# An attention and mixture-of-experts layer: heads in row groups of 32 partitions, the first batch projected in place, and the experts' down projections as plain fp32 matmuls

## The reference

```python
Q, K, V = (proj(Wq, bq), proj(Wk, bk), proj(Wv, bv))        # 16 heads of 8
scores = jnp.einsum('bhqd,bhkd->bhqk', Q, K) * scale
attn = jax.nn.softmax(scores, axis=-1)
...
shared_out = jax.nn.silu(xf @ sw1) * (xf @ sw3) @ sw2
s = jax.nn.sigmoid(xf @ router_w.T)                          # top 2 of 8, gates from s
h = jax.nn.gelu(jnp.einsum('nd,edh->neh', xf, ew1), approximate=False)
y = jnp.einsum('neh,ehd->ned', h, ew2)
routed_out = jnp.einsum('ned,ne->nd', y, comb)
```

## Time and profile before

| | us |
|---|---|
| median of the three timed runs | 265.02 (263.12 to 265.13) |
| span of the profiled execution | 261.9 |
| what lies outside the span, if the median is taken | 3.1 |
| first score matmul | 42.58 |
| last probabilities-times-v matmul ends | 172.7 |
| last down matmul ends | about 253.2 |
| TensorE busy | 225.9 (86%) |
| VectorE busy | 186.1 (71%) |
| ScalarE busy | 152.3 (58%) |
| GpSimd busy | 119.1 (45%) |

### The profile page before, as it was taken

One profiled execution on the slowest core, in us unless ns is written; L12 is line 12 of the kernel. 1 busy time (PEld: TensorE's weight loads), 2 busy tenths in 40 slices (PEclk: granted clock), 3 DMA queues, 4 the chain that ended last, 5 costly groups with the idle time before them and its releaser, 6 DMA issues.

```text
span 261.9 us, 4502 instructions
## 1 busy us (share of the span) xinstructions
PE 225.9 (86%) x1546; PEld 158.7 (61%) x1546; DVE 186.1 (71%) x370; ACT 152.3 (58%) x292; POOL 119.1 (45%) x186
## 2 busy tenths in 40 slices
PE   1766984999999999994999999997999899999850
PEld 1434854667677677772676766655767576767520
DVE  8953893777969879794269762348567796976953
ACT  1440722576666667663356678866696468665620
POOL 8677381000100007130448988435319977273511
PEclk9995885899999999999589999999979999999995
DMA  7277864405528082476000000069980495792111
GB/s 191 53 92 91 86 69 98 40 11 86 45 53 77 23 85 30 78 53 228 3 0 5 3 5 5 4 108 140 226 143 28 94 147 84 129 161 74 40 40 40
DMA packets 16198, 19.43 MB, mean 74 GB/s; under 512 B 1280, under 2 KB 11712, under 8 KB 16032
## 3 DMA queue, kind: packets, MB, share of 16 engines
q1 hardware_dynamic: 15744, 18.49, 43.4%
q0 software_dynamic: 144, 0.39, 1.0%
q10 hardware_dynamic: 288, 0.27, 0.6%
HBM read 11.22 MB, written 1.11 MB: 47 GB/s over the span
## 4 chain that ended last, share of the span: by engine, by line
PE 59%; DMA 13%; DVE 11%; POOL 6%; issue 5%; ACT 3%; SPq 1%; POOLq 0%; DVEq 0%; ACTq 0%
PE ring L818 17%; PE pv_bank L832 14%; PE max_bank L804 12%; DMA kstack<-gate_scratch 6%; DMA qstack<-top_rows 4%; POOL qstack L522 3%; DVE kstack L629 3%; DVE probs_mem L737 2%; DMA kstack<-qk_parts 2%; ACT qstack L556 1%; PE misc_bank L871 1%; PE misc_bank L882 1%; PE max_bank L788 1%; PE max_bank L789 1%; PE max_bank L790 1%
## 5 line engine op out<-in xcount | busy, mean ns | idle before, releaser
L669 DVE TENSOR_REDUCE top<-max_bank 128x2 f32<-128x512 f32 x128 | 84.0, 684 | 32.9 <-PE max_bank L804 31.7
L569 ACT ACTIVATE probs_mem<-ring 128x512 f32<-128x512 f32 x128 | 73.9, 597 | 43.6 <-PE ring L818 42.4
L818 PE MATMUL ring<-qstack,kstack 128*128 128x256 f32 x256 | 62.9, 331 | 7.7 <-DMA qstack<-top_rows 7.7
L818 PEld LDWEIGHTS ring<-qstack,kstack 128*128 128x128 f32 x256 | 40.5, 199 | 35.9 <-ACT probs_mem L569 25.1
L804 PE MATMUL max_bank<-kstack,qstack 128*128 128x256 f32 x256 | 56.5, 312 | 3.6 <-DMA kstack<-qk_parts 3.3
L804 PEld LDWEIGHTS max_bank<-kstack,qstack 128*128 128x128 f32 x256 | 43.0, 209 | 7.7 <-DMA kstack<-qk_parts 4.1
L832 PE MATMUL pv_bank<-probs_mem,v 128*18 128x256 f32 x512 | 41.3, 397 | 0.0
L737 DVE TENSOR_TENSOR probs_mem<-probs_mem,kstack 128x512 f32<-128x512 f32 x32 | 24.8, 798 | 11.9 <-POOL qstack L522 6.2
L556 ACT CAST qstack<-probs_mem 128x512 fp32r<-128x512 f32 x32 | 19.7, 615 | 16.5 <-DVE probs_mem L737 16.2
L522 POOL TENSOR_TENSOR qstack<-probs_mem,qstack 128x512 fp32r<-128x512 f32 x14 | 19.5, 1392 | 16.2 <-ACT qstack L556 16.1
L473 POOL TENSOR_SCALAR rstd<-mv 128x2 f32<-128x2 f32 x8 | 1.8, 226 | 48.7 <-DVE mv L706 48.5
(11 more groups left out here) (146 smaller groups left out, 386.6 us busy)
## 6 DMA issues: line engine op xcount, KB each, us to landing
kstack<-gate_scratch SPq DMA_DIRECT2D x4, 2048.0 KB, 15.5
kstack<-qk_parts SPq DMA_DIRECT2D x24, 64.0 KB
wf<-w_ffn_dram SPq DMA_DIRECT2D x1, 1408.0 KB, 5.8
qstack<-qk_parts SPq DMA_DIRECT2D x9, 128.0 KB
xs<-x_dram SPq DMA_DIRECT2D x4, 256.0 KB, 5.2
out_dram<-xs SPq DMA_DIRECT2D x4, 256.0 KB, 2.3
kstack<-wf_hi SPq DMA_DIRECT2D x12, 64.0 KB
qstack<-wf_hi SPq DMA_DIRECT2D x6, 128.0 KB
```

Source lines behind the costliest of these rows:

```text
L569: nc.scalar.activation(probs[:, k // 2 % 4, c % 2 * 512:(c % 2 + 1) * 512], ring[k % NRING][:, :], ACT.Exp, scale=SCALE).then_inc(probs_ma ...
L669: dve.tensor_reduce(top[:, half, h:h + 3:2], max_bank[n % NMAX][:, :].rearrange("p (h k) -> p h k", h=2), AX.X, ALU.max).then_inc(max_take ...
L818: ins = mm(ring[k % NRING][:, j * S:(j + 1) * S], kstack[:, s, ab, r, kt * P:(kt + 1) * P], qstack[:, s, r, :], start=True, stop=True)
```

## The change

Four things change together.

1. **Heads in row groups.** Each head now takes 26 rows in one of four row groups of 32 partitions: 8 rows q high, 8 rows q high, 8 rows q low, 2 rows for the shift, against k high, k low, k high, ones. `qstack` and `kstack` are `[128, 4, 2048]`, one place for every token, so nothing is recycled and nothing has to be zero. A score matmul contracts over 26 rows and a maxima matmul over 24. In a tick, head c's scores and head (c + 2) % 4's maxima are issued in turn. `times_v` runs once in a tick instead of twice. `LEAD` is 4.
2. **Shift by two ticks.** The maxima go to the stacks after every two steps instead of after every four: 16 times, each with 4 DMAs (one for each row group) instead of 8 times with 2.
3. **First batch in place.** Batch 0 is projected with weights (`w_first`) whose columns are laid out like the stack's rows, so ACT and DVE write its stack directly. Batch 1 is unit 1 (256 tokens), then come three units of 512 tokens. A unit is spread into the stacks by 24 DMAs (`spread`; 32 KB each for unit 1, 64 KB each after it), by SP and, for the q half of unit 1, by GpSimd. The projections of the last two units stand in ticks 1, 2, 7 and 8. `wf` is loaded at tick 1, gates 0 and 1 at ticks 21 and 30.
4. **Down projections in fp32.** The product of an expert step goes straight to one fp32 matmul; the casts, the low parts and two of the three matmuls go away. `LAG` is 2 and the product has three buffers.

```diff
-LEAD = 6
-NSLOT = 4
+LEAD = 4
+GR = 3 * HD
+KROWS = GR + 2
+UNITS = [(0, S), (S, S)] + [(g * GT, GT) for g in range(1, NG)]
+COPIES = (((0, 1), (HD, 0), (2 * HD, 0)), ((0, 0), (HD, 0), (2 * HD, 1)))
...
+        for n in range(2 * NB):
+            jobs[2 * n + 2 - LEAD, 0].insert(0, ("shift", n))
+        for u, tick in ((2, -1), (3, 3), (4, 9)):
+            for n in range(2 * HPS):
+                jobs[tick + n // 2, n % 2].append(("stack", (u, 1 - n // HPS, n % HPS)))
...
+        jobs[1, 1].append(("load w", 0))
...
-            jobs[max(UP0 + 1, EX0 + NE * (g - 1)), 1].append(("load gates", g))
+            jobs[(21, 30, EX0 + NE, EX0 + 2 * NE)[g], 1].append(("load gates", g))
...
+        def spread(eng, u, i, j):
+
+            t0, n = UNITS[u]
+            for r, part in COPIES[i]:
+                wait_parts(eng, u, i, part)
+                eng.dma_start(stacks[i][32 * j + r:32 * j + r + HD, :, t0:t0 + n].bitcast(F32),
+                              parts[(u - 1) % 2][32 * j:32 * j + 32, i, part, 0:n].bitcast(F32)).then_inc(
+                                  stack_loaded[u] if u > 1 or i else q1_loaded, 16)
...
                     if kind == "shift":
-
                         wait_taken(sp, (kind, b))
-                        for ab in range(NAB):
-                            move(qstack[32 * ab:32 * ab + 2, b % NSLOT, :, :],
-                                 top_rows[16 * ab:16 * ab + 16, b % 2, :]).then_inc(shift_loaded[b % 2], 16)
-                        if b == 0:
-                            stack(3)
+                        t, q = b % 2 * 2, b // 2 * S
+                        for j in range(HPS):
+                            move(qstack[32 * j + GR:32 * j + KROWS, t:t + 2, q:q + S],
+                                 top_rows[4 * j:4 * j + 4, b % 2, :]).then_inc(shift_loaded[b % 2], 16)
...
+                    if kind == "first":
+                        bank = first_bank[b]
+                        act.wait_ge(first_proj, b + 1)
...
+                        for i in range(2):
+                            nc.scalar.activation(first_hi[:, i, :], bank[:, i * S:(i + 1) * S], ACT.Identity,
+                                                 bias=b1[:, i * NT + b:i * NT + b + 1]).then_inc(first_hi_made, 1)
...
+                        for i in range(2):
+                            nc.scalar.activation(first_lo[:, b % 2, i, :], first_hi[:, i, :].bitcast(F32), ACT.Identity,
+                                                 scale=lo_rows[:, i:i + 1]).then_inc(first_lo_made, 1)
...
+            def scores(i, c, kt):
+
+                (b, t), r = batch_tile(i), slice(32 * c, 32 * c + KROWS)
+                ins = mm(ring[(4 * i + c) % NRING][:, kt * S:(kt + 1) * S], kstack[r, t, b * S + kt * P:b * S + (kt + 1) * P],
+                         qstack[r, t, b * S:(b + 1) * S], start=True, stop=True)
...
+            def maxima(i, c, qt):
+
+                (b, t), j = batch_tile(i), (c + 2) % HPS
+                r = slice(32 * j, 32 * j + GR)
...
-                        pe.wait_ge(lo_made[n % 2], n // 2 + 1)
-                        c = slice(E2 + e * P, E2 + (e + 1) * P)
-                        three(acc, wf_hi[:, c], wf_lo[:, c], hid_hi[:, b % 4, :], hid_lo[:, b % 4, :],
-                              False, e == NE - 1).then_inc(down_made, 1)
+                        pe.wait_ge(hid_made, n + 1)
+                        mm(acc, wf[:, E2 + e * P:E2 + (e + 1) * P], hid[:, n % NHB, :], start=False,
+                           stop=e == NE - 1).then_inc(down_made, 1)
```

More of the change, by code:

```diff
@@ L30 @@
 QT = S // P
-NAB, NPAIR = 2, 8
+NT = 4
 HPS = 4
@@ L409, in _ @@
                         load_gates(b)
-                if half and step(tick) and tick % SPB == 3 and tick // SPB + NSLOT < NB:
-                    stack(tick // SPB + NSLOT)
-                    if tick // SPB + NSLOT == NB - 1:
-                        for b in (NB - 2, NB - 1):
-                            wait_stack(sp, b)
-                        sp.dma_start(wf[:, :], w_ffn[:, 0:RW]).then_inc(wf_loaded, 16)
             sp.wait_ge(out_stored, 16 * NG)
@@ L800, in maxima, with wait_for_maxima @@
+            def wait_for_maxima(i, c):
+                (b, t), n = batch_tile(i), 4 * i + c
+                if b == 0 and c == 0:
+                    pe.wait_ge(first_done, 2 * t + 2)
+                if b and t == 0 and c == 0:
+                    wait_spread(pe, unit_of(b))
                 if n >= NMAX:
                     pe.wait_ge(max_taken, n - NMAX + 1)
-                for j in range(2):
-                    ab, r = heads[2 * (c % 2) + j]
-                    ins = mm(max_bank[n % NMAX][:, j * S:(j + 1) * S], qstack[:, s, r, qt * P:(qt + 1) * P],
-                             kstack[:, s, ab, r, :], start=True, stop=True)
@@ L836, in times_v @@
-                if kt == QT - 1:
-                    ins.then_inc(pv_made, 1)
+                pe.wait_ge(probs_made, 4 * (i + 1))
+                for kt in range(QT):
+                    for j in range(HPS):
+                        ins = mm(pv_bank[32 * j:32 * j + 2 * VW, 0:S],
+                                 v[:, (QT * b + kt) * H // 2 + HPS * n + j, k * VW:(k + 2) * VW],
+                                 probs[:, i % 2, j, kt * S:(kt + 1) * S],
+                                 start=(k == 0 and kt == 0), stop=(k == 1 and kt == QT - 1))
@@ L839, in _ @@
+                ins.then_inc(pv_made, 1)
             pe.wait_ge(ident_set, 1)
-            for n in range(PRE):
-                project(n)
             for tick, half in HALVES:
@@ L844, in _ @@
                     if step(tick):
-                        scores(tick, c)
+                        wait_for_scores(tick, c)
+                        scores(tick, c, 0)
                     if step(tick + LEAD):
-                        maxima(tick + LEAD, c)
-                    if step(tick - 1) and c % 2 == 0:
-                        times_v(tick - 1, half)
+                        wait_for_maxima(tick + LEAD, c)
+                        maxima(tick + LEAD, c, 0)
+                    if step(tick):
+                        scores(tick, c, 1)
+                    if step(tick + LEAD):
+                        maxima(tick + LEAD, c, 1)
+                    if step(tick - 1) and c == 1:
+                        times_v(tick - 1)
                 for kind, b in jobs[tick, half]:
```

547 lines of the change are left out of this document (256 added, 291 removed), and 5 rows, old and new, of the table jobs.

## The result

The changed kernel takes **291.81 us** (median of 4 runs, 289.93 to 296.89); the kernel before, on the same chip, 264.65 (263.12 to 265.13). The ratio is 1.101, 95% interval 1.093 to 1.109: 10% slower, where 1.9% faster was forecast. The profiled execution took 290.25 us with a span of 288.5, and TensorE's mean granted clock fell from 0.931 to 0.810.

The account below looks back on a forecast made before the run. It took the chain of waits as ending on DMAs before the first score, with PE busy without a gap in attention. Span 261.9 - 14.6 + 12.6 - 3.0 = 256.9, plus 3.1 to the median: 260.0 us, range 246 to 276.

Parts of the forecast that it names:

- Part B: Attention, from the first score to the last times_v: 142.7 us against 130.1 before, +12.6.
- 7.2 us for two ticks: Attention loop from matmuls through transposes, copy, four SP issues and landing to the next scores: 6.9 to 7.4, taken as 7.2.
- clock again: Attention walk: after the stall before tick 4, PE's clock costs time once more, putting tick 6 at 61.0 us.
- the free pace: Attention without stalls: 3.6 us a tick instead of 3.95, 14 x 7.2 + 13 = 114 us in all.
- the stalls: Attention delays from SP's in-order issues and queued transfers, longest at ticks 4 and 24: some 29 us of Part B.
- PE's share of a loop: Two attention ticks: eight matmuls at 0.92 or 0.46 us, two times_v of 0.56, less one mode change: 1.7 to 2.2.
- Part A: Start of the kernel to the first score: 28 us, between 25 and 31, a gain of 14.6 us.
- Part C: Feed-forward after attention: expert pace stays, gain 0 to 1 us, tail gains 2.5; sum -3.0, between +3 and -6.
- Weight loads do not bind: Rival denied here: in attention, weight loads bind and row groups bring no overlap; 262 to 268 us, chance 0.2.
- The slower rival: SP's order and DMA queues hold attention back more, at ticks 2 to 14 and gates 0: 267 to 276 us, chance 0.28.

Follow-up runs that it names:

- experiment 2: Changed kernel without the 64 shift DMAs and the waits for them: 289.72 us, ratio 1.096.
- experiments 3 and 5: Changed kernel with two extra 128-row matmuls per score/maxima group: 304.39 us; maxima in the same head's row group: 305.21 us; all in one row group: 332.86 us.
- the halves: Changed kernel with times_v in two halves, behind the second and fourth score groups of a tick, instead of whole behind the second: 272.11 us, ratio 1.029.
- experiment 6: Changed kernel with times_v in two halves: 272.11 us; also without shift DMAs: 262.87 us; kernel before with times_v whole behind the second score group: 266.92 us.

## Why the prediction was wrong

The forecast was 260.0, between 246 and 276, with 0.27 for slower; the time was 291.8.

- **The step that failed is Part B's pace.** It let PE's clock go to half only after a stall and return within one pair of ticks ("clock again"), so that 7.2 us for two ticks held nearly throughout. Measured, 120 us of attention ran at a mean of 0.70; it does so without a stall (experiment 2), and the clock falls without a gap (experiments 3 and 5). The premise was that a clock seen at 1.00 with 128-row matmuls would be granted to 24-row ones. No row of the trace before could show that, and I gave it neither a bound nor a rival. Part B was 168.9 for 142.7: of the 31.8 us beyond my number it makes 26.2, the start 5.75. That 26.2 is the difference of two larger errors, and that they offset each other is luck: the free pace was put at 114 us for the stretch and was about 159 (168.9 less 10.1 of PE's waits for transfers), +45; the stalls were put at 29 and were 10.1, -19. (The prediction's terms for PE's share of a loop add up to 1.6 to 2.0 us before the change of mode, not 1.7 to 2.2; that is 0.1 to 0.2 us in 7.2.)
- **The free pace was right where its premises held:** 3.5 us a tick with the halves at full clock, and the overlap as sized (0.055 a matmul; I had 0.46 for eight of them, measured 0.44). **That the order of `times_v` matters was missed.** I costed its passes, not its place. At full clock the changed kernel's ticks take 3.9 us instead of 3.5, which over 28 ticks is an estimated 11 us; what the place cost in all was 19.7 us, together with the clock; at 128 rows 3.
- **The stalls were found and sized in the right place, but in the wrong kernel.** With full rows five waits of 20.4 us, of the 29 that I had (which count unit 2's as well); in the changed kernel 8.3. I added stalls to a pace that was PE's own at full clock; at half clock most of them are hidden.
- **Part A, 28 us, came at 33.75.** Its sum followed ACT. PE was late instead: the chain of waits has two groups of fp32 projections of 2.00 us and three jobs of unit 2 of 1.7 to 2.0 ahead of the first score.

```profile
12.47 2.00 PE pv_bank L825 x4
...
16.06 2.02 PE ring L825 x4
...
26.06 1.71 PE misc_bank L832 x2
...
28.49 2.00 PE misc_bank L832 x2
...
31.22 2.00 PE misc_bank L838 x8
```

  Such a group takes 0.88 when PE is at full clock (in the run over 128 rows the second one, at 22.34), so PE was at the lower level here too, although the clock column reads 1.00 up to 34 us.
- **Part C, -3.0, came at -3.3,** for the stated reasons. The tail is shorter: the last up matmul starts at 276.41 and the last down one ends at 279.39, 3.0 us where it was 6.0 (247.25 to 253.24). The pace holds: eight down projections in a row, 225.56 to 236.46, stand 1.56 us apart, as summed:

```profile
225.56 1.02 PE L924 MATMUL max_bank<-probs_mem,wf 128*128 128x512 f32 x2
227.12 1.02 PE L924 MATMUL max_bank<-probs_mem,wf 128*128 128x512 f32 x2
228.68 1.02 PE L924 MATMUL max_bank<-probs_mem,wf 128*128 128x512 f32 x2
```

- **The rivals.** Weight loads do not bind: the trace has four loads and matmuls in 0.22 us. By the Trainium skill's price for a load (page TensorE: Matmul & The Clock Gate, section LDWEIGHTS (loading the stationary operand); its formula gives about 107 ns for 128 columns) four of them, taken one after the other, would need an estimated 0.43. The slower rival named the right sign and the wrong place: queues were to hold attention back, and the run without the shift shows that its transfers did not, in this kernel.
- **Open.** How few rows a matmul may have, and what share of the time, before the clock falls: 64 rows gave 0.84, and a mix of two 128-row matmuls to four short ones 0.80. Whether it is the rows or the values in them: the runs over 64 and 128 rows feed PE other numbers as well. Also why the order moves the clock by so much at equal work; that waits for exp make long half-clock stretches likelier fits experiment 6, but was not separated from the time that they cost themselves.

## What to carry to other kernels

Packing heads into row groups makes the matmuls overlap, but PE's clock is part of the price: before sizing such a change, ask what runs at full clock now because tall matmuls keep it there, and give "same schedule at half clock" as a rival with its own time. Measure the same schedule with all rows and again with every matmul in one row group: neither overlaps, so the two differ in rows and clock and in little else. When an edit of a suspected stall changes nothing, try it again with the larger loss removed (0 to 2 us against 19 here), and cost the place of a long step in the order, not only its length.

## What the hardware showed that was not expected

- With 24 to 26 rows in one row group the granted clock stood at 0.50 from 140 to 160 us with PE busy 20.00 of 20.00 us; in the run with the filler it went from 1.00 to 0.50 while PE was busy 2.00 of every 2.00 us. With 128 rows, without the shift, it stood at 1.00 from 80 to 200 us.
- Four matmuls of 256 columns in four row groups, with their weight loads, take 0.22 us at full clock, 0.055 each; one by one in one group 0.12 each.
- The clock column read 1.00 in the first 34 us of the changed kernel, while fp32 groups took 2.00 us that take 0.88 at full clock: the durations are the check on it.
- Some kernels with a falling clock scatter (258.15 to 268.72, 326.07 to 349.12 us) and some don't: the one with the lowest clock, 0.57, has 319.24 to 321.79.
